# First edge stage of a graph kernel: centred rows squared on ScalarE, scaled there two groups late, and one factor prepared in the node pass

## The reference

```python
x = _layernorm(x + _L0_gnn_ref(x, edge_attr_48, src, dst, eps))   # relu(x[src] + edge), summed by dst, + (1+eps) x
x = _layernorm(x + _L1_gnn_ref(x, edge_weight, src, dst))         # 10 steps of f = 0.9 * sum_by_dst(f[src] * w) + 0.1 * x
x = _layernorm(x + _L2_gnn_ref(...))
x = _layernorm(x + _L3_gnn_ref(...))
# _layernorm(x) = (x - mean) / sqrt(var + 1e-5)
```

## Time and profile before

| what | us |
|---|---|
| median of the runs | 4838.02 (4836.48 to 4844.4) |
| span of the profiled execution | 4790.5 |
| median less span | 47.5 |
| node pass, 252 to 745 (VectorE busy 447.6) | 493 |
| first edge stage, 889 to 1582 (VectorE busy 595.8, TensorE 517.0, GpSimd 382.9, ScalarE 208.0) | 693 |

### The profile page before, as it was taken

How to read it: one execution, slowest core, us unless ns; L and a number is a source line. 1 busy time by engine, 2 the same in 40 slices (tenths; PEclk the granted TensorE clock), 3 DMA queues, 4 the chain that set the end, 5 groups by cost and what they waited for, 6 DMA issues and landing times. The chain is left out here.

```text
span 4790.5 us, 62717 instructions
## 1 busy us (share of the span) xinstructions
PE 2834.2 (59%) x9882; PEld 1512.3 (32%) x9882; DVE 3044.4 (64%) x7896; ACT 1274.6 (27%) x3949; POOL 2839.4 (59%) x2768
## 2 busy tenths in 40 slices
PE   4700000477777799999999948664222200996664
PEld 2500000133333366666666622211111100333332
DVE  8989992588888577777777748642333235664333
ACT  0023330132332244444444412111100001442111
POOL 0067777555555177767777766475655540665776
PEclk9955555687777799999999969877555555996555
DMA  2057773799999566679999857622433323232111
GB/s 67 0 160 213 219 214 84 117 181 176 177 176 166 151 169 165 168 157 165 167 170 167 161 111 210 156 71 53 61 49 46 42 55 102 66 72 46 38 37 28
DMA packets 751644, 578.92 MB, mean 121 GB/s; under 512 B 497075, under 2 KB 660092, under 8 KB 746564
## 3 DMA queue, kind: packets, MB, share of 16 engines
q1 hardware_dynamic: 593672, 429.40, 35.4%
q0 software_dynamic: 97280, 106.57, 19.3%
q10 hardware_dynamic: 60612, 42.15, 4.7%
HBM read 282.82 MB, written 301.55 MB: 122 GB/s over the span
## 5 line engine op out<-in xcount | busy, mean ns | idle before, releaser
L488 POOL DMA_INDIRECT xdst<-in_x,dstc x400 | 459.4, 1149 | 401.1 <-PEq L637 260.9
L1252 POOL DMA_INDIRECT out<-xob,ob x400 | 438.6, 1096 | 236.2 <-DVE xob L1366 134.8
L272 POOL DMA_INDIRECT gb<-nodes,ib x400 | 391.1, 978 | 292.7 <-ACT ib L845 192.7
L261 PE MATMUL bank<-ident,act 128*99 128x128 f32 x400 | 87.3, 357 | 782.1 <-DVE act L989 717.9
L272 POOL DMA_INDIRECT parent<-upper_rows,ib x400 | 392.0, 980 | 189.3 <-issue 121.6
L292 PE MATMUL bank<-chosen,rec 128*6 128x512 bf16 x1200 | 375.8, 479 | 0.9 <-DVE chosen L279 0.9
L272 POOL DMA_INDIRECT cgb<-layer,ib x160 | 169.6, 1060 | 258.6 <-ACT ib L2144 212.1
L261 PEld LDWEIGHTS bank<-ident,act 128*99 128x99 f32 x400 | 66.2, 224 | 790.5 <-issue 790.5
L1288 PE MATMUL bank<-hm,w 128*112 128x512 f32 x600 | 300.8, 640 | 0.0
L266 PE MATMUL bank<-ident,scan 99*128 99x99 f32 (+2 forms) x1120 | 198.9, 307 | 156.0 <-DVE scan L1957 101.5
L1305 PE MATMUL bank<-bxT,w 121*128 121x512 f32 x600 | 276.7, 597 | 10.7 <-ACT bxT L1198 10.7
(11 more groups left out here) (296 smaller groups left out, 7227.7 us busy)
## 6 DMA issues: line engine op xcount, KB each, us to landing
nodes<-wt SPq DMA_DIRECT2D x40, 1286.2 KB
edges<-gb ACTq DMA_DIRECT2D x100, 194.0 KB
run_rows<-tb SPq DMA_DIRECT2D x100, 194.0 KB
upper_rows<-tb SPq DMA_DIRECT2D x100, 194.0 KB
xa<-upper_rows SPq DMA_DIRECT2D x100, 194.0 KB
parent_rows<-parent SPq DMA_DIRECT2D x100, 194.0 KB
kb<-edge_keep SPq DMA_DIRECT2D x100, 192.0 KB
lsb<-edges SPq DMA_DIRECT2D x200, 96.0 KB
```

The costliest lines, as they stand in the source:

```text
L261: last = nc.tensor.transpose(slot(dst_ps[0:w, :], t), rows_sb[:, t, c0:c0 + w], ident[:, :])
L272: yield nc.gpsimd.indirect_dma_start(out=dst[s][:, t, 0:width], out_offset=None, in_=table, in_offset=bass.IndirectOffsetOnAxis(ap=ib[s][: ...
L488: nc.gpsimd.indirect_dma_start(out=xdst[:, k * F:(k + 1) * F], out_offset=None, in_=a["x"], in_offset=bass.IndirectOffsetOnAxis(ap=dstc[:, ...
L1252: nc.gpsimd.indirect_dma_start(out=out, out_offset=bass.IndirectOffsetOnAxis(ap=ob[s][:, t:t + 1], axis=0), in_=xo[s][:, t, :], in_offset= ...
```

## The change

Four things change in the edge stage and one in the node pass.

- `eq` is no longer computed by VectorE. ScalarE squares `ed` (`run_square`, in its body behind `from_rows`), and VectorE sums the squares behind its `scan` (`run_spread`).
- `tb`'s scaled rows are no longer computed by VectorE. ScalarE does them with four activations of 128 x 48 (`run_scale`), at the front of its body two groups later, with the reciprocal as scale. `ed` and `er` get two buffers each; VectorE writes `ed` of group g only when the scaling of group g - 2 is done.
- SyncE waits for one semaphore more ahead of the two stores of `tb` (`s_pos`).
- The weight `wl` is one multiplication in place of two: the comparison with the flag is gone, and so is the wait for the flag.
- In the node pass the factor in column NW - 3 is already zero for a node that is not lone. It comes from another instruction form, and the 1 + ALPHA is taken into the epsilon of the root.

```diff
@@ node pass: ScalarE, then VectorE second_rows
-  root(s_v2, s_s2, nv2, ns2, (1 + ALPHA) ** 2)
+  root(s_v2, s_s2, nv2, ns2, 1.0, eps_keep)        # eps_keep = LN_EPS / (1 + ALPHA) ** 2
-  nc.vector.tensor_scalar(wt[s][:, :, NW - 3], ns2[:, :], 1.0 / (1 + ALPHA), None, ALU.mult)
-  ch[4].then(nc.vector.scalar_tensor_tensor(out=nr2[:, :], in0=nr2[:, :], scalar=1 + ALPHA, in1=nr1[:, :], op0=ALU.mult, op1=ALU.mult))
+  nc.vector.scalar_tensor_tensor(out=wt[s][:, :, NW - 3], in0=node_pos[:, bass.ds(n * ROWS, ROWS), 0], scalar=0.0, in1=ns2[:, :], op0=ALU.is_equal, op1=ALU.mult)
+  ch[4].then(nc.vector.tensor_tensor(nr2[:, :], nr2[:, :], nr1[:, :], ALU.mult))
@@ edge stage: SyncE store
   sp.wait_ge(s_tb, g + 1)
+  sp.wait_ge(s_pos, g + 1)
@@ edge stage: ScalarE
+  def run_square(i, s):
+      g = i * U + s
+      act.wait_ge(s_cen, g + 1)
+      wait(act, s_evar, g)
+      nc.scalar.activation(eq[:, :, :], ed[s % 2][:, :, :], ACT.Square).then_inc(s_sq, 1)
+
+  def run_scale(i, s):
+      g, b = i * U + s, s % 2
+      act.wait_ge(s_er, g + 1)
+      for t in range(T):
+          last = nc.scalar.activation(tb[b][:, t, 0:F], ed[b][:, t, :], ACT.Copy, scale=er[b][:, t:t + 1])
+      last.then_inc(s_tb, 1)
+
   def body(i, s, end=None):
+      part(run_scale, i, s, 2, end)
       part(relued, i, s, 0, end)
       part(from_rows, i, s, 1, end)
+      part(run_square, i, s, 1, end)
       part(run_std, i, s, 1, end)
       part(unpack, i, s, 3, end)
@@ edge stage: VectorE run_end
-  spread(epi, ey[:, :, :], ed[:, :, :], eq[:, :, :], em[:, :], T)
-  nc.vector.tensor_reduce(eu[:, :], eq[:, :, :], AX.X, ALU.add).then_inc(s_evar, 1)
+  epi.then(nc.vector.tensor_reduce(em[:, :], ey[:, :, :], AX.X, ALU.add))
+  wait(dve, s_tb, g - 1)
+  nc.vector.scalar_tensor_tensor(out=ed[s % 2][:, :, :], in0=mid(em[:, :], T), scalar=-1.0 / F, in1=ey[:, :, :], op0=ALU.mult, op1=ALU.add).then_inc(s_cen, 1)
+
+  def run_spread(i, s):
+      dve.wait_ge(s_sq, i * U + s + 1)
+      nc.vector.tensor_reduce(eu[:, :], eq[:, :, :], AX.X, ALU.add).then_inc(s_evar, 1)
@@ edge stage: VectorE run_end_x1 (L965 now also increments s_pos)
   dve.wait_ge(s_estd, g + 1)
-  epi.then(nc.vector.reciprocal(er[:, :], es[:, :]))
-  nc.vector.tensor_tensor(tb[b][:, :, 0:F], ed[:, :, :], mid(er[:, :], T), ALU.mult).then_inc(s_tb, 1)
+  nc.vector.reciprocal(er[b][:, :], es[:, :]).then_inc(s_er, 1)
@@ edge stage: VectorE body
-  dve.wait_ge(s_fl, g + 1)
-  weight.then(nc.vector.scalar_tensor_tensor(out=wl[:, :], in0=fl[s][:, :], scalar=0.0, in1=col(w9, g), op0=ALU.is_equal, op1=ALU.mult))
-  weight.then(nc.vector.tensor_tensor(wl[:, :], wl[:, :], gb[s][:, :, NW - 3], ALU.mult))
+  weight.then(nc.vector.tensor_tensor(wl[:, :], col(w9, g), gb[s][:, :, NW - 3], ALU.mult))
@@ behind the scan of group g
   if begun(i, s, 1):
+      run_spread(*back(i, s, 1))
       run_end_x1(*back(i, s, 1))
```

More of the change, by code:

```diff
@@ L167, in gnn @@
         eps100 = sb("eps100", [P, 1])
+        eps_keep = sb("eps_keep", [P, 1])
         zrow = sb("zrow", [1, TW])
@@ L406, in _ @@
                     nc.vector.memset(eps100[:, :], 100 * LN_EPS)
+                    nc.vector.memset(eps_keep[:, :], LN_EPS / (1 + ALPHA) ** 2)
                     nc.vector.memset(zrow[:, :], 0.0)
@@ L664, in square, with root @@
                         nc.scalar.activation(nq[b][:, :, :], nd[b][:, :, :], ACT.Square).then_inc(s_done, 1)
-                    def root(i, s, s_in, s_done, of, to, scale):
+                    def root(i, s, s_in, s_done, of, to, scale, eps=lneps):
                         act.wait_ge(s_in, i * U + s + 1)
-                        nc.scalar.activation(to[:, :], of[:, :], ACT.Sqrt, bias=lneps[0:HP, :], scale=scale).then_inc(s_done, 1)
+                        nc.scalar.activation(to[:, :], of[:, :], ACT.Sqrt, bias=eps[0:HP, :], scale=scale).then_inc(s_done, 1)
                     def load(i, s):
@@ L691, in body @@
                         part(lambda *at: root(*at, s_v4, s_s4, nv4, ns4, 1.0 / F), i, s, 4, end)
-                        part(lambda *at: root(*at, s_v2, s_s2, nv2, ns2, (1 + ALPHA) ** 2), i, s, 3, end)
+                        part(lambda *at: root(*at, s_v2, s_s2, nv2, ns2, 1.0, eps_keep), i, s, 3, end)
                         part(ends_of, i, s, 3, end)
@@ L786, in gnn @@
             base = slots("base", [1, 1], I32, n=U, scope=scope)
-            ey, ed, eq = (scope.enter_context(nc.sbuf_tensor(n, [P, T, F], F32)) for n in ("ey", "ed", "eq"))
-            wl, em, eu, er, es, place = (
-                scope.enter_context(nc.sbuf_tensor(n, [P, T], F32)) for n in ("wl", "em", "eu", "er", "es", "place"))
+            ey, eq = (scope.enter_context(nc.sbuf_tensor(n, [P, T, F], F32)) for n in ("ey", "eq"))
+            ed, er = st("ed", F), slots("er", [P, T], n=2, scope=scope)
+            wl, em, eu, es, place = (
+                scope.enter_context(nc.sbuf_tensor(n, [P, T], F32)) for n in ("wl", "em", "eu", "es", "place"))
             psT, psR, psC = bank[0:2], [wide(z, MW) for z in bank[2:4]], bank[4:6]
@@ L795, in gnn @@
             (s_stage, s_add, s_fl, s_relu, s_m1, s_cols, s_scan, s_rows, s_sum, s_cr, s_rec, s_hot, s_pack, s_packed, s_lw,
-             s_tb, s_weight, s_epi, s_evar, s_estd, s_kt) = (scope.sem(f"a_{n}") for n in (
+             s_tb, s_weight, s_epi, s_cen, s_sq, s_evar, s_estd, s_er, s_pos, s_kt) = (scope.sem(f"a_{n}") for n in (
                  "stage", "add", "fl", "relu", "m1", "cols", "scan", "rows", "sum", "cr", "rec", "hot", "pack", "packed",
-                 "lw", "tb", "weight", "epi", "evar", "estd", "kt"))
+                 "lw", "tb", "weight", "epi", "cen", "sq", "evar", "estd", "er", "pos", "kt"))
             s_zero = scope.sem("a_zero")
@@ L946, in _ @@
                 def _(dve):
-                    weight, epi = Chain(dve, s_weight, 2), Chain(dve, s_epi, 5)
+                    weight, epi = Chain(dve, s_weight, 1), Chain(dve, s_epi, 2)
                     for z in rec:
@@ L964, in run_end_x1 @@
                         dve.wait_ge(s_cr, 2 * (g + 1))
-                        nc.vector.scalar_tensor_tensor(out=tb[b][:, :, 2 * F], in0=cr[b][:, :, 0], scalar=0.0, in1=cr[b][:, :, 2], op0=ALU.is_gt, op1=ALU.mult)
+                        nc.vector.scalar_tensor_tensor(out=tb[b][:, :, 2 * F], in0=cr[b][:, :, 0], scalar=0.0, in1=cr[b][:, :, 2], op0=ALU.is_gt, op1=ALU.mult).then_inc(s_pos, 1)
                         wait(dve, s_lw, 16 * (g - U + 1))
@@ L1004, in _ @@
                     run_end(NT - 1, U - 1)
+                    run_spread(NT - 1, U - 1)
                     run_end_x1(NT - 1, U - 1)
```

## The result

The changed kernel takes 4854.8 us (median of 5 runs, 4847.8 to 4855.65), the kernel before 4838.02 (5 runs, 4834.72 to 4844.4). The ratio is 1.0033, 95% interval [1.0021, 1.0046]: 16.8 us slower. Forecast were 4834 us, and slower with a chance of 0.27.

The account below looks back on a forecast made before the run. The prediction took full DMA engines (share 1.10 at 176 GB/s) to bound the edge stage. It summed 4838 - 4 (quiet stretch) - 2 (startup, drain) + 1 (last group) + 1 (node pass) = 4834 us, range 4785 to 4885.

Parts of the forecast that it names:

- the landing does not get shorter: Edge stage, `tb` loop: longer own part, stores landing no sooner, 7.15 us a group, 4870 us (4899 at worst); chance 0.25.
- The root: Edge stage: a DMA share of 1.10 at 176 GB/s means the 16 DMA engines are full.
- VectorE's saving: Edge stage: shorter steps save VectorE 1.33 us a group, so 6.39 would become 5.06.
- a pace of 5 us a group: Edge stage: VectorE would need 5.06 us; the no-DMA-limit rival had 5.35 to 6.1 a group, chance 0.06.
- The loop's own part: Edge stage, `tb` loop: from ScalarE's copy to the end of row scaling, growing from 2.37 to 3.6 us.
- The sign by which that rival was to be known: Edge stage: rate under 174 GB/s with waits over 2 us a group at the `tb` copy; chance 0.25.
- The node pass: Factor's instruction from 0.186 to at most 0.240 us, 1 us in all; pass within 2 us of its 493.
- the first line of the sum: Edge stage: VectorE gives up 1.3 us, DMA takes it; 6.67 to 6.84, taken as 6.75 us a group.
- the third rival: Edge stage, `tb` loop: landing does not get shorter, kernel slower at 4870 us; chance 0.25.
- with less outstanding they shorten: Edge stage: argument against the 0.25 rival; landings are late because the DMA is full, and shorten with less outstanding.
- The four scalings: Edge stage, ScalarE: four 128x48 scalings cost 0.76 to 1.48 us a group, taken as 0.85.
- So 47.5 us lie outside the span: Whole kernel: median 4838.02 less profile span 4790.5 leaves 47.5 us outside the span, taken as unchanged.

Follow-up runs that it names:

- e18: Changed kernel loading only the first 64 of 512 mask columns after the first turn, so fewer bytes; 0.5% under the kernel before, 6.71 us a group.
- the pair on one chip: Kernel before and changed kernel, both with the flags' store issued by ScalarE instead of SyncE, on one chip: 4800.38 and 4814.35 us.
- e9: Kernel before with the flags' store issued by ScalarE instead of SyncE; 4800.38 us where the kernel before takes 4809.53.
- e10: Changed kernel with the flags' store issued by ScalarE instead of SyncE; 4814.35 us where the kernel before takes 4809.53.
- e17: Changed kernel with four `tb` buffers instead of two, on a quick chip; 1.0002 of the kernel before, 7.00 us a group.
- e12: Changed kernel with SyncE's packed list issued ahead of the two row stores, where the kernel before takes 4809.53 us; 6.94 us a group.
- e1_before_again: Kernel before, unchanged, profiled anew on a chip of the slow kind; 8.1 us a group.

## Why the prediction was wrong

The time, 4854.8 us, lies in the range of 4785 to 4885. The direction was forecast wrong: the changed kernel is slower, which had 0.27, and the rival with 0.25, "the landing does not get shorter", comes nearest. It is right in the sign, the waits and the rate, and only in part in the place, as the four buffers show below.

**What held.** The root: VectorE's saving is worth nothing where the DMA share is over 1. VectorE's work fell by 1.03 us a group (0.9 forecast), ScalarE's rose by 1.18 (1.1 to 1.9), the share is 1.12 (1.10 to 1.15), and a pace of 5 us a group was never near. Run e18 says it from the other side: bytes taken away shorten the group. ScalarE waits at the `tb` copy in the whole stage and VectorE at `eu`. The loop's own part is 3.77 us on average (3.6 forecast), the landing 10.6 (10.7 in that rival), and the group 7.2 (7.15), though 6.98 in the pair on one chip. The sign by which that rival was to be known came as put down: under 174 GB/s (167) with waits of over 2 us a group at the copy (2.2). The node pass runs from 268.5 to 738.1 by its first and last `nx`, 268.4 to 739.4 before. Its factor takes 196 ns, in this group of the changed kernel:

```profile
L761 DVE SCALAR_TENSOR_TENSOR wt<-node_pos,ns 125x20 f32<-125x20 f32 x33 | 6.5, 196 | 4.7 <-DVE nr L760 4.5
```

**The step that failed** is the first line of the sum, "VectorE gives up 1.3 us a group, and the DMA takes it: at 180 GB/s a group is 1.200 / 0.180 = 6.67 us". It took the rate of a stretch for a ceiling that only bytes divide by. The rate is a result: at shares of 1.09 to 1.13 it was 176, 177, 167, 173 and 172 GB/s (before, e9, after, e10, e17) with the same bytes. So a group did not go from 6.81 to 6.75 us but got longer. The two profiles put it at 7.21, which would be 68 x 0.40 = 27 us for the quiet stretch alone, more than the 16.8 of the whole kernel. The pair on one chip puts it at 6.83 and 6.98: 95 groups x 0.15 = 14 us, by an estimate from these two, and 14.0 were measured between them.

**The argument that failed with it** stood against the third rival: "with less outstanding they shorten". It rests on a loop of 2.37 us of its own and a landing of 11.3. The first leaves out waits inside the loop: over the 18 copies of that stretch the two are 2.65 and 10.8. The change made the loop's own part 1.1 us longer, and the landings gave back 0.2 of it (10.6).

**Four buffers** take the wait at the copy away, and a group still takes 7.00 us at 172 GB/s, as in e10 and e12 with the wait, on another chip of the quick kind. So, by these three, the wait is where the slower transfers are felt first, not what sets the 7.0. The edge stage of e17 (882.6 to 1578.4 by the first and last `msg`) is 15 us longer than that of e9 (887.7 to 1568.7), and 1 us longer than that of e10 (887.1 to 1581.7). That its kernel is level with before all the same (1.0002) is only partly seen. Its stage starts 5 us sooner than e9's, the next stage's first-to-last `x3d` is 7 us shorter (1145.5 for 1152.9), and e9 is itself 0.15% faster than the kernel before. The plain changed kernel did not run on that chip, so it is not shown that the two buffers cost the 0.3%.

**Sizes.** The four scalings were taken as 0.85 us and took 1.01; a single one takes 0.32, nearer the large tile than the small, yet one starts before the last has ended. "So 47.5 us lie outside the span": 1.8 do. This did no harm to the sum, which used differences, but it moved the profile of before away from the runs it was set against, and the two profiles' edge stages (678 and 722 us) differ by 44, the runs by 17. In the pair on one chip the stages are 681 and 695 us, and the medians differ by 14. The other 30 us are then most likely those of the two executions or their chips, not of the change.

**Open.** What makes the packets take longer: the order of the `run_rows` and `edges` stores is a guess that fits. The parts of the change one by one, where a group takes 7 us; whether the packed list, whose every transfer waits for the one before it, would be a pace of its own with a lower DMA share; and why some chips take 8 us a group. The quickest version with all of the work in it is the kernel before with its flags' store on ScalarE: 0.9985 [0.9976, 0.9995], against 1.0002 for the changed kernel with four buffers.

## What to carry to other kernels

Where the DMA share stays over 1, work taken off a compute engine bought no time. Look instead at what the change does to the stores: here two of them changed places, the rate fell from 177 to 173 GB/s at the same bytes, and the group grew by 0.15 us. Don't divide bytes by the rate of a full stretch to get a ceiling; look at what each kind of packet takes. A wait at a buffer says where the slow transfers are felt: two buffers more took it away here and the group stayed at 7.0 us, so try the buffers before you call the wait the cause. Run before and after on one chip for the profiles too, and set a profile's span against its own execution's time, not against the median.

## What was not expected of the hardware

A `run_rows` packet of 388 bytes took 0.025 us before and 0.059 after (0.028 and 0.048 in the pair on one chip), with nothing changed in the transfer itself, and an `edges` packet of the same size went from 0.052 to 0.037. The one of the two stores that leaves second had the longer packets in each of the six profiles above. The DMA share hardly showed it (1.10 and 1.12).

Chips differ more than most changes do: the kernel before took 4809 to 4838 us on some and 5493 to 5563 on others. On the latter a group took 7.5 to 8.4 us at a DMA share of 0.72 to 0.94, and the same change went from 0.33% slower to 0.8% faster on one (0.9918 [0.9890, 0.9945]) and to no clear change on another (0.9977 [0.9946, 1.0009]). The slow chips are slower in more than this stage: in `e1_before_again` the last `msg` starts at 1682.2 (1568.7 in e9), and 3808 us follow it (3236 in e9). A packet of the gather, 4116 bytes, took 0.49 us there and 0.35 in the first profile.
